# Cross network in a recommendation tower: units from SBUF for every tile, another order of the first tile's second layer, and a later split of the third tile

## What is computed

```python
for W in (W0, W1, W2):                       # 64 units each
    Wr = W.reshape(24, H_prev, 64)
    Xk = einsum('bfd,bhd,fho->bod', e, Xk, Wr)   # Xk = e before the first layer
    outs.append(Xk.sum(axis=2))              # sum over d
z = concatenate(outs, axis=1)                # B x 192
h = relu(concatenate([z, dense_ctx]) @ W_top1 + b_top1)
y = relu(h @ W_top2 + b_top2) @ W_top3
```

## Time and profile before

| | us |
|---|---|
| runs before, median of 3 | 585.45 |
| lowest, highest | 584.02, 591.72 |
| the profiled execution | 578.03 |
| its span, first to last instruction | 576.2 |

### The profile page before, as it was taken

The page is one execution under the profiler, slowest core; times in us unless marked ns, Lnnn a source line. Parts: engine busy times, 40 slices in busy tenths (PEclk is TensorE's granted clock), DMA queues, the critical chain, the costliest instruction groups (busy, mean ns, idle before and its releaser), DMA issues.

```text
span 576.2 us, 7709 instructions
## 1 busy us (share of the span) xinstructions
PE 370.3 (64%) x3000; PEld 168.8 (29%) x3000; DVE 307.3 (53%) x305; ACT 137.1 (24%) x282; POOL 187.3 (33%) x196
## 2 busy tenths in 40 slices
PE   0010200856088439726998269755999998999995
PEld 0010000212022115302452025212553553553554
DVE  1010001473278347643789348526799798798930
ACT  1000000001022113302333123303253353251253
POOL 6777773027506720672017700771000000000000
PEclk9999999977779759976999869777999999999999
DMA  6000100191436326721757246702756847848300
GB/s 163 6 7 7 7 7 4 41 252 29 98 107 150 86 60 190 211 57 40 190 165 188 45 123 186 197 7 63 227 160 173 222 139 195 221 140 208 90 1 1
DMA packets 28039, 64.30 MB, mean 112 GB/s; under 512 B 7311, under 2 KB 10823, under 8 KB 28012
## 3 DMA queue, kind: packets, MB, share of 16 engines
q1 hardware_dynamic: 21868, 62.35, 40.3%
q0 software_dynamic: 6144, 1.59, 3.0%
HBM read 53.86 MB, written 5.85 MB: 104 GB/s over the span
## 4 chain that ended last, share of the span: by engine, by line
another core or an unknown queue 33%; PE 24%; DMA 14%; DVE 11%; issue 8%; ACT 4%; POOL 4%; SPq 2%; DVEq 0%; ACTq 0%
PE acc L622 14%; DVE pairs L416 8%; DMA units<-x_dram 5%; DMA turned<-x_dram 5%; POOL emb L388 4%; PE spread L596 2%; DMA x_dram<-common 2%; PE misc L683 1%; ACT x0diag L489 1%; DVE z L421 1%; SPq L328 1%; ACT x0parts L476 1%; DVE rest L284 1%; DMA units<-x 1%
## 5 line engine op out<-in xcount | busy, mean ns | idle before, releaser
L416 DVE TENSOR_TENSOR pairs<-spread,units 128x1024 f32<-128x1024 f32 x192 | 225.9, 1218 | 118.3 <-remote 76.4
L388 POOL DMA_INDIRECT emb<-in_tbl,ids_sb x192 | 187.1, 975 | 203.2 <-DVE parts L288 143.6
L622 PE MATMUL acc<-pairs,w_sb 128*64 128x512 f32 x768 | 205.2, 642 | 4.4 <-DVE pairs L416 4.3
L596 PE MATMUL spread<-x0parts,sel 72*64 72x512 bf16 (+1 forms) x280 | 50.6, 450 | 116.9 <-ACT common L476 39.6
L622 PEld LDWEIGHTS acc<-pairs,w_sb 128*64 128x64 f32 x768 | 53.3, 146 | 76.0 <-issue 54.3
L416 DVE TENSOR_TENSOR pairs<-turned,common 120x1024 f32<-120x1024 f32 x42 | 51.1, 1220 | 24.6 <-DMA turned<-x_dram 24.6
L596 PEld LDWEIGHTS spread<-x0parts,sel 72*64 72x64 bf16 (+1 forms) x280 | 14.6, 121 | 159.3 <-ACT common L476 71.4
L643 PE MATMUL misc<-ident_b,parts 128*72 128x128 bf16 x120 | 11.7, 253 | 67.0 <-DVE parts L288 36.9
L622 PE MATMUL acc<-pairs,w 120*64 120x512 f32 x180 | 49.6, 636 | 2.4 <-DVE z L421 2.1
L416 DVE TENSOR_TENSOR pairs<-spread,common 120x1024 f32<-120x1024 f32 x6 | 7.3, 1223 | 68.9 <-remote 65.1
L476 ACT ACTIVATE x<-acc 128x512 f32<-128x512 f32 x31 | 18.7, 602 | 96.8 <-PE acc L622 80.2
(11 more groups left out here) (57 smaller groups left out, 192.6 us busy)
## 6 DMA issues: line engine op xcount, KB each, us to landing
units<-x_dram SPq DMA_DIRECT2D x56, 512.0 KB, 6.2
turned<-x_dram SPq DMA_DIRECT2D x42, 480.0 KB
units<-x SPq DMA_DIRECT2D x16, 256.0 KB, 5.1
x_dram<-x SPq DMA_DIRECT2D x28, 128.0 KB
emb<-in_tbl,ids_sb POOLq DMA_INDIRECT x192
x_dram<-common SPq DMA_DIRECT2D x14, 96.0 KB
x_dram<-common SPq DMA_DIRECT2D x14, 56.0 KB
w_sb<-in_w SPq DMA_DIRECT2D x2, 384.0 KB
```

What stands on the lines that cost most here:

```text
L388: pool.indirect_dma_start(out=e3[:, f, :], out_offset=None, in_=tables[f], in_offset=bass.IndirectOffsetOnAxis(ap=ids_sb[:, t, f:f + 1], a ...
L416: dve.tensor_tensor(pairs[buf][0:rows, :], source[0:rows, :], other[0:rows, h * HALF:(h + 1) * HALF], ALU.mult).then_inc(pairs_done, 1)
L596: last = pe.matmul(spread[ring][lo:hi, half * BLK:(half + 1) * BLK], sel[:, first + lo:first + hi], src[:, cols(h, half)], start=True, sto ...
L622: last = pe.matmul(acc[half * H:(half + 1) * H, :], w, pairs[buf][0:rows, half * BLK:(half + 1) * BLK], start=first, stop=final)
```

## The change

Four things are changed.

- `units` of every tile are loaded from `x1` in SBUF, as tile 0's were. The stores of x1 to DRAM, their semaphore, and the waits of ACT for them (`x1_read`) are gone.
- SP's queue is no longer laced: for tile t it has x0 and `turned` of both halves, then the units of both halves.
- Step 0 starts with the items (g, j) = (0,0), (1,0), (0,1), (1,1), and so on up to (1,3), where it had (0,0) to (0,3), (1,0) to (1,3). The side work `xt` moves from the places 6 and 8 to 5 and 7, and the first `common` from 10 to 9.
- Tile 2 (the third) is split at place 28 of step 0, where it had been at 24. So the gather of tile 4 is released there.

```diff
+L2_FIRST = [("L2", g, j, 0) for j in range(UNIT_GROUPS) for g in range(2)] + L2_ITEMS[2 * UNIT_GROUPS:]
...
-    def __init__(self, l1_at=(), common_at=(), common_slot=(), side=(), splits={}):
+    def __init__(self, l1_at=(), common_at=(), common_slot=(), side=(), splits={}, order=L2_ITEMS):
         self.side, self.splits, self.common_at = dict(side), splits, common_at
-        rest = iter(L2_ITEMS)
+        rest = iter(order)
...
-SIDE_FIRST = {6: ("xt", 0), 8: ("xt", 1), 22: ("x0t", 0)}
+SIDE_FIRST = {5: ("xt", 0), 7: ("xt", 1), 22: ("x0t", 0)}
...
-FIRST = Plan((17, 19, 21, 24, 25, 26), (10, 13), (1, 0), SIDE_FIRST, {4: 1, 24: 2})
+FIRST = Plan((17, 19, 21, 24, 25, 26), (9, 13), (1, 0), SIDE_FIRST, {4: 1, 28: 2}, L2_FIRST)
...
-            def store_x1(t, h):
+            def load_units(t, h):
 
                 sp.wait_ge(x1_done, 2 * t + h + 1)
-                for half in range(2):
-                    sp.dma_start(x1_dram[h][:, half * BLK:(half + 1) * BLK], x1[half * H:(half + 1) * H, h, :])\
-                        .then_inc(x1_stored, 16)
-
-            def load_units(t, h, js):
-
-                sp.wait_ge(x1_stored, 64 * (t - 1) + 32 * (h + 1))
-                for j in js:
+                for j in range(UNIT_GROUPS):
                     if t >= 2:
 
                         last = MIDDLE.items.index(("L2", FIELD_GROUPS - 1, j, h))
                         sp.wait_ge(pairs_done, item(t - 2, last) + 1)
-                    rows = x1_dram[h][j:H:UNIT_GROUPS, :].rearrange("v (u c) -> v u c", u=1)
-                    sp.dma_start(units[t % 2][:, j, h * HALF:(h + 1) * HALF], rows.to_broadcast([UNITS, FIELDS, HALF]))\
-                        .then_inc(units_in[t % 2][h][j], 16)
...
                     for half in range(2):
                         rows = x1[half * H + j:(half + 1) * H:UNIT_GROUPS, h, :].rearrange("v (u c) -> v u c", u=1)
-                        sp.dma_start(units[0][:, j, h * HALF + half * BLK:h * HALF + (half + 1) * BLK],
-                                     rows.to_broadcast([UNITS, FIELDS, BLK])).then_inc(units_in[0][h][j], 16)
+                        sp.dma_start(units[t % 2][:, j, h * HALF + half * BLK:h * HALF + (half + 1) * BLK],
+                                     rows.to_broadcast([UNITS, FIELDS, BLK])).then_inc(units_in[t % 2][h][j], 16)
...
-            for h in range(2):
-                first_units(h)
-            store_x0(1, 0)
-            load_turned(1, 0, range(L1_CHUNKS))
+            load_units(0, 0)
+            load_units(0, 1)
             for t in range(1, TILES):
-
-                store_x0(t, 1)
-                load_turned(t, 1, range(L1_CHUNKS))
-                store_x1(t, 0)
-                load_units(t, 0, range(UNIT_GROUPS))
-                store_x1(t, 1)
...
+                for h in range(2):
+                    store_x0(t, h)
+                    load_turned(t, h, range(L1_CHUNKS))
+                for h in range(2):
+                    load_units(t, h)
...
-                        dve.wait_ge(units_in[slot][h][j], (i - slot) * 8 + 16 * (2 - slot))
+                        dve.wait_ge(units_in[slot][h][j], (i - slot) * 16 + 32)
...
             def take_x1(last_item, tile, h, bank):
 
-                x1_read(act, tile, h)
 
                 act.wait_ge(main_done, last_item + 1)
```

More of the change, by code:

```diff
@@ L184, in build_tower @@
         x0_dram = [nc.dram_tensor(f"x0_dram{h}", (X0_ROWS, HALF), F32).ap() for h in range(2)]
-        x1_dram = [nc.dram_tensor(f"x1_dram{h}", (H, HALF), F32).ap() for h in range(2)]
         spread = [ctx.enter_context(nc.psum_tensor(f"spread{s}", [P, HALF], F32)) for s in range(2)]
@@ L207, in build_tower @@
         turned_in = [sem(f"turned_in{c}") for c in range(L1_CHUNKS)]
-        x1_stored = sem("x1_stored")
         units_in = [[[sem(f"units_in{s}_{h}_{j}") for j in range(UNIT_GROUPS)] for h in range(2)] for s in range(2)]
@@ L317, in load_units @@
                         sp.wait_ge(pairs_done, item(t - 2, last) + 1)
-                    rows = x1_dram[h][j:H:UNIT_GROUPS, :].rearrange("v (u c) -> v u c", u=1)
-                    sp.dma_start(units[t % 2][:, j, h * HALF:(h + 1) * HALF], rows.to_broadcast([UNITS, FIELDS, HALF]))\
-                        .then_inc(units_in[t % 2][h][j], 16)
-            def first_units(h):
-                sp.wait_ge(x1_done, h + 1)
-                for j in range(UNIT_GROUPS):
                     for half in range(2):
                         rows = x1[half * H + j:(half + 1) * H:UNIT_GROUPS, h, :].rearrange("v (u c) -> v u c", u=1)
-                        sp.dma_start(units[0][:, j, h * HALF + half * BLK:h * HALF + (half + 1) * BLK],
-                                     rows.to_broadcast([UNITS, FIELDS, BLK])).then_inc(units_in[0][h][j], 16)
+                        sp.dma_start(units[t % 2][:, j, h * HALF + half * BLK:h * HALF + (half + 1) * BLK],
+                                     rows.to_broadcast([UNITS, FIELDS, BLK])).then_inc(units_in[t % 2][h][j], 16)
             def store_x0(t, h):
@@ L526, in take_common @@
                 copy(common[:, h * HALF:(h + 1) * HALF], spread[buf][0:COMMON_ROWS, :]).then_inc(common_done, 1)
-            def x1_read(eng, tile, h):
-                if isinstance(tile, int) and tile == 1:
-                    for j in range(UNIT_GROUPS):
-                        eng.wait_ge(units_in[0][h][j], 32)
-                elif not isinstance(tile, int) or tile > 1:
-                    eng.wait_ge(x1_stored, 64 * (tile - 2) + 32 * (h + 1))
             def take_x1(last_item, tile, h, bank):
-                x1_read(act, tile, h)
                 act.wait_ge(main_done, last_item + 1)
```

## The result

Over 20 executions each, beside each other on one chip, the changed kernel has a median of 590.13 us (586.81 to 597.67), the kernel before 585.15 (578.68 to 593.72). The ratio is 1.012, with a 95% interval of 1.010 to 1.015: a small loss where a gain of 1.1% was forecast, and above the forecast's range, which ended at 588.5.

A forecast was written before the change was run, and what follows sets the result against it. Bound: windows of back-to-back gathers, each costing PE 17 to 20 us, plus a PE otherwise nearly full. Terms −2.8 + 0 + 0 − 2.8 − 1 = −6.6 us off the 585.45 median gave 578.9 us, range 565.0 to 588.5.

The forecast's parts named there:

- the units' step: Units from SBUF in all tiles: −2.8 us after 430 and −1 us in all gather windows together.
- DVE's waits for `turned`: DVE's 9.0 us of these waits after 425 were taken as hidden by PE's backlog: 0, at most those 9.0.
- 112 smaller loads in place of 56: Unit loads of 256 KB for 512 KB: no cost, since issuing keeps up and pairs land every 2.0 us.
- windows of one price: Each stretch of 24 indirect gathers in a row for one tile costs PE 17 to 20 us.
- its test for this: If the forecast is right, PE still idles 16 to 20 us in each gather window.
- a sign of being wrong: A gather window in which PE idles under 10 us or over 25: windows then have no fixed price.
- The first tile's order: First step, two field groups per unit group: split and all that follows, first gather window included, 2.8 us earlier.
- rival 2: First gather window: DVE sticks at item 8 waiting for PE's third spread, +9.8 us, 588.7 us in all; chance 0.12.
- The later split: Third tile split at place 28, so the second gather window begins 5.3 us later: 0, between −5.3 and +5.3.
- Rival 1: Second gather window loses less, as ACT's copies get through first: 9.8 us fall away, 569.1 us; chance 0.24.
- Rival 3: Little happens: gather windows swallow the 2.8 us, and only the end gives 2.8 us, 582.7 us; chance 0.12.

The follow-up runs named there:

- `l_lead`: Changed kernel with DVE held at each split of place 20 until PE has contracted item 18; 591.85 us, ratio 1.016 to the kernel before.
- `i_halves`: Kernel before with each unit group loaded from DRAM by two transfers of 256 KB instead of one of 512 KB; 588.12 us, ratio 1.007.
- `c2_units`: Kernel before with only the units of all tiles from SBUF and SP's queue unlaced, on chip 9; 591.45 us, ratio 1.011.
- `m_best`: Changed kernel with the gathers from the third tile on spaced, mostly 24 over 29 items, by waits on DVE's products; 481.17 us, ratio 0.826.

## Why the prediction was wrong

**What failed: the units' step.** It was to give −2.8 behind 430 and −1 in the windows. The first came, with −3.6 from the sixth step on: the gaps of 2.41 and 0.78 us are down to 0.40 and nothing. But the part as a whole made +6 us on chip 9 (591.45 against 585.01), where the forecast had −3.8. Two terms of it were mis-sized:

- "DVE's waits for `turned` (...) were hidden by PE's backlog: 0." Hidden they were, and for that they held DVE back at no cost to PE. Of 24.6 us of such waits 3.3 were left, DVE came to the fourth opening three items ahead of PE where it had been one ahead, and a window that opens so lets through 10 items where it had let through 14.5. `l_lead` shows the link from lead to items. That the lost waits made the lead is read from the traces: the four with waits of 5.2 us or more ahead of the fourth opening have a lead of 1 to 2.5 there, those with less and no hold have 3 or more. How much of the 6 us this is isn't shown, since a hold by hand cost as much as it gave, and another price of the copies out of SBUF under a window is not ruled out.
- 112 smaller loads in place of 56 cost 0, as they land fast enough. No wait of DVE for units was left behind the first tile, but `i_halves` puts 0.7% on such loads (588.12 against 583.32 us, interval 0.2 to 1.2%), some 1.3 to 7 us.

**What failed beneath it: windows of one price.** The forecast took a window at 17 to 20 us of PE time whatever falls into it, and only its last release as decisive. The release was as steady as forecast: 34.4 to 34.7 us behind the opening in the fourth window of all three kernels shown. But the work that PE gets done until then goes from 7 to 14.5 items in these traces, which the forecast held fixed. The prediction named idle times as its test for this; PE is idle for 17.1, 21.9, 16.6, 18.2 and 18.1 us of the five times 34.5 in the changed kernel, close to the forecast of 16 to 20 but for the second (in `c2_units` the second has 25.4, just beyond the 25 that the prediction named as a sign of being wrong). What PE lost it lost at a lower clock more than in gaps: in the fourth window it was busy 16.3 us for 10 items, where it had been 18.4 us for 14.5, at a mean granted clock of 0.70 instead of 0.89, that is, for longer at the lower of its two levels.

**The first tile's order: right up to the first window.** −2.8 forecast, −2.4 in the trace: the opening at 123.09, forecast 122.7, and PE's last long idle ended at 158.81, forecast 158. DVE waited 2.30 us for PE's third spread, so rival 2 (it sticks at item 8, +9.8) didn't occur. Whether it shortens the whole is not shown: alone it left the median where it was (584.61 against 585.01), and in the whole change nothing of it is seen.

**The later split: 0 by the medians, as forecast; but not as argued.** In the changed kernel's trace the second window opened at 179.60 (forecast near 178), ACT stuck at x2's copy for 18.46 us and at `common` until 214.31, and PE got 7 items done in 34.5 us (28 matmuls of the contraction line) where it had done 11 (44). That is the loss that the bounds allowed (up to 5.3) rather than the 0 between them. With the split alone moved, the first two stretches together grew from 107.9 to 112.1 us in the trace, and no later one made up for it (67.4, 59.1 and 216.7 against 67.1, 58.8 and 216.9). Yet the median stayed (584.81 against 585.01), with a ratio of 1.002 (0.998 to 1.007): one trace of each can't settle it, and a small loss stays possible.

**Rivals.** Rival 1 (the second window loses less) is the reverse of what came. Rival 3 (the windows swallow the gain) comes nearest and stopped short at 582.7: it let windows swallow a gain, but not grow by more. None of the three let the windows become dearer through an engine that was no longer held back. The one that was missing: a wait that is hidden today may be what keeps two engines in step when a window opens.

## What to carry to other kernels

Before a hidden wait is put down at nothing, look at what the waiting engine releases next, and in which state the other engines will be found: here DVE, no longer held, opened the next burst of gathers with PE's backlog still unserved. And where a trace shows one engine's burst slowing all others, spread the burst over the work first; a single wait per gather on the progress of DVE gave 11 to 17% in five kernels, against the 1% that the reordering around it moved. Measure such a kernel on more than one chip before ranking its edits, since the units' part of this one is a loss on chip 9 and a gain on chip 13.

## What was not expected of the hardware

- The same program took 432 us on chip 13 and 583 to 585 on the chips 1, 9 and 12, as in the result's own runs. The difference is the windows: on chip 13 no wait ends on "remote", PE was busy 278 of 280 us in the units' variant, and the gathers of the tiles 3 to 7 cost 5 us instead of 123. Why chips differ is open.
- What a burst of gathers takes from ACT and DVE is open too. They are issued 1.25 us apart (0.94 us and 0.31 idle), and the last held-up release comes 34.4 us after the first of 24, so 1.43 us per gather, as if something served them at that rate and the releases stood behind them. Spreading 24 of them over 29 or 30 items takes most of the cost away (496.25 and 481.17 us for 591), which fits; no run showed what it is.
- PE counts as busy for longer in the slower kernel: 381.3 us in the changed kernel, 361.1 in `m_best`, with the same 3000 matmuls. The mean granted clock is 0.88 in the one and 0.97 in the other.
